# Two passes in one turn of the loop, with no barrier between them: counting semaphores, waits on the producers, and an order table over both passes

## The chip, the cores and the metric

The kernel runs on one core of one Trainium2 chip, in one launch. The metric is the device time in microseconds (us). The core's engines are named PE (TensorE, the matrix engine; its weight loads are PEld), DVE (VectorE), ACT (ScalarE), POOL (GpSimd) and SP (SyncE, which issues the DMAs here). Each engine runs its own stream of instructions in order and waits for the others by semaphores.

## The reference

The input is a batch of 32 independent samples of 256 tokens by 256 features, in float32. Each goes through two decoder layers, every sublayer behind a layer norm and added to the residual:

```
x = x + L0_attn (ln(x))                  # 16 heads of 16, low-rank k and v, rotary over heads   -> stream m
x = x + L0_xattn(ln(x), ctx, ctx)        # 16 heads of 64; softmax over the heads of a token     -> stream h
x = x + L0_ffn  (ln(x))                  # top half of the tokens by a router, FFN 1024, gate    -> stream h
x = x + L1_attn (ln(x))                  # 16 heads, keeps the top 25 of 256 scores of each row  -> stream t
x = x + L1_xattn(ln(x), ctx, ctx, lens)  # 16 heads of 16 over ctx, keys beyond lens masked      -> stream c
x = x + L1_ffn  (ln(x))                  # one product with a ternary weight                     -> stream c
```

## The kernel before, in words

All weights stay in SBUF. A sample (256 tokens by 256 features, two tiles of 128 tokens) passes through four **streams**, one per pass: m (attention of layer 0), h (cross attention over heads, router and FFN), t (the top-25 attention), c (masked cross attention, ternary FFN). A pass runs all four streams at once, each on another sample: m on i+3, h on i+2, t on i+1, c on i. With 32 samples there are 3 filling passes, 29 full ones in a loop of the hardware (`nc.Fori`, L1155), and 3 draining ones. The functions `tensor_h`, `vector_t`, `scalar_c`, `pool_m` and so on hold one engine's share of one stream, as Python generators with a `yield` at the points where another stream may come in. The function `woven` draws them together by a table of letters, `ORDER`, one string per engine: this table alone fixes the order of the instructions on each engine.

Within a pass the engines meet at named semaphores (`g["mla_x"]` is counted when stream m's residual is written, `spa_x` for stream t's, `md_x3` for stream h's, `lin_o` for stream c's). A pass ends with all engines at the end of an `nc.Block`, and a second block in which SP sets all the semaphores back to zero; a value waited for is the same in every pass. Streams hand samples on through buffers: m writes `xin`, which h reads next; h writes `xa`, which t reads next; t writes `x4`, which c reads next. Streams c and m share three PSUM banks (`bankM`) and the buffers of attention (`bufM`), so m follows c in a pass; h has `bankH`, t has `bankT`.

Lines used below: L299 transposes of a layer norm's output, L546 the projections of stream h (the first, `xwv`, from `ctxA`), L314 and L322 projections from and onto 256 features (`cwk`, `cwv` from `ctxB` are stream c's first, `swo` into `bankT` is stream t's last), L340 the scores, L350 their row maxima, L391/L394/L421 the transposed scores and values of streams m and c with the exponentials on ACT (L408), L883/L887 the 8-by-8 maxima and their removal (stream t's top 25), L863 the first DVE step of stream t after its layer norm, L529 the additions to the residual, L274/L278/L291 layer norm on DVE, L480 the reciprocals of a stream's attention sums, L1107 and L1145 the ends of the blocks.

## Time and profile before

| | us |
|---|---|
| median of 3 runs (6767.83, 6768.36, 6782.65) | 6768.36 |
| the profiled execution, its own time | 6756.82 |
| its span | 6755.0 |
| busy in that span: PE / DVE / ACT / POOL | 5896.7 / 4510.2 / 4012.6 / 1507.3 |
| mean granted clock of TensorE, as a share of 2.4 GHz | 0.899 |

Busy times overlap between engines. Busy PE is time in which a matmul was under way, whatever the clock; a matmul at the lower clock (1.2 GHz) counts longer. DMA hardly matters: 54.18 MB in the whole span, most at its start.

### The profile page before, as it was taken

To read this page: it belongs to the slowest core of one execution; us is meant where nothing else is said; L and a number is where in the kernel's file an instruction comes from. 1 tells how busy PE (TensorE), PEld (TensorE's weight loads), DVE (VectorE), ACT (ScalarE), POOL (GpSimd) and SP (SyncE) were. 2 spreads that over 40 slices of the span, in tenths; PEclk is the share of its full clock that TensorE was granted. 3 is DMA by queue.
4 is the path that set the end of the run, shared out by engine and by line. 5 is a ranking of instruction groups with operands and counts; after the bars stand their busy time and mean duration, and the time that the engine had idled before them with its cause. 6 is when DMAs were issued, how large, how long until landed. Compare 5 with 4: busy or idle time off the path is not lost. (4 is left out here: it accounts for less than half of the span.)

```text
span 6755.0 us, 109667 instructions
## 1 busy us (share of the span) xinstructions
PE 5896.7 (87%) x37509; PEld 3877.2 (57%) x37762; DVE 4510.2 (67%) x16186; ACT 4012.6 (59%) x9761; POOL 1507.3 (22%) x2564
## 2 busy tenths in 40 slices
PE   6888988988988988898888898888898898898876
PEld 3565565565565565565565565566556556556542
DVE  1366766666777666776676676666776666677653
ACT  2465666565666665666656566656566655566632
POOL 0122222222222222222222222222222222222211
PEclk7789989899999899999999899999998999999965
DMA  2000000000000000000000000000000000000000
GB/s 79 4 6 6 4 8 6 8 8 6 4 8 7 6 8 6 4 8 8 6 8 6 6 6 8 6 8 7 7 4 8 6 8 8 6 4 8 4 2 5
DMA packets 29456, 54.18 MB, mean 8 GB/s; under 512 B 8145, under 2 KB 9810, under 8 KB 27986
## 3 DMA queue, kind: packets, MB, share of 16 engines
q1 hardware_dynamic: 28770, 45.73, 2.1%
q8 instruction: 345, 5.65, 0.3%
q14 instruction: 341, 2.79, 0.1%
HBM read 37.33 MB, written 8.39 MB: 7 GB/s over the span
## 5 line engine op out<-in xcount | busy, mean ns | idle before, releaser
L914 POOL TENSOR_TENSOR t_pr<-t_pr,sc 128x512 f32<-128x512 f32 x512 | 649.6, 1269 | 1495.9 <-ACT t_pr L839 1495.9
L350 DVE TENSOR_REDUCE m_nm<-bankM 128x2 f32<-128x512 f32 x1024 | 657.0, 683 | 347.9 <-PE bankM L340 344.0
L887 DVE MATCH_REPLACE8 wk<-m,wk 128x256 f32<-128x256 f32 x2048 | 821.0, 408 | 0.0
L340 PE MATMUL bankM<-m_kT,m_q 32*128 32x256 f32 x4096 | 698.5, 466 | 75.4 <-DVE m_nm L350 74.3
L883 DVE MAX8 m<-wk 128x8 f32<-128x256 f32 x2048 | 759.2, 412 | 0.0
L651 ACT ACTIVATE xk_area<-bankH,xb 64x256 f32<-64x256 f32 x1024 | 480.7, 469 | 460.4 <-PE bankH L546 438.1
L394 PE MATMUL bankM<-m_q,m_kT 32*128 32x512 f32 x2048 | 627.9, 691 | 0.0
L883 DVE MAX8 m<-sc 128x8 f32<-128x256 f32 x1024 | 380.0, 412 | 327.5 <-ACT sc L830 290.1
L340 PEld LDWEIGHTS bankM<-m_kT,m_q 32*128 32x128 f32 x4096 | 411.3, 216 | 312.4 <-DVE m_nm L350 133.6
L845 ACT ACTIVATE t_pr<-t_pr,t_nm 128x256 f32<-128x256 f32 x1024 | 463.9, 504 | 182.5 <-POOL t_pr L914 180.5
L408 ACT ACTIVATE m_pT<-bankM,keymask 128x512 f32<-128x512 f32 x512 | 323.7, 683 | 247.4 <-PE bankM L394 247.4
L546 PE MATMUL bankH<-ctxA,xwv 128*128 128x256 f32 x1024 | 312.4, 467 | 166.2 <-issue 155.2
L445 ACT ACTIVATE t_pt<-bankT 128x512 f32<-128x512 f32 x512 | 307.5, 601 | 235.7 <-PE bankT L436 228.7
L391 PE MATMUL bankM<-m_m,sel_b 128*128 128x512 bf16 x865 | 301.2, 418 | 158.3 <-ACT m_pT L408 136.7
L436 PE MATMUL bankT<-ident,t_pr 128*128 128x128 f32 x2048 | 384.3, 318 | 55.4 <-ACT t_pr L845 54.3
L908 POOL TENSOR_SCALAR mx<-m 128x2 f32<-128x2 f32 x512 | 112.9, 221 | 1431.3 <-DVE wk L887 1421.1
L408 ACT ACTIVATE m_pT<-bankM 128x512 f32<-128x512 f32 x512 | 277.1, 593 | 235.3 <-PE bankM L394 235.3
L887 DVE MATCH_REPLACE8 wk<-m_last,wk 128x256 f32<-128x256 f32 x1024 | 410.5, 408 | 0.0
L887 DVE MATCH_REPLACE8 wk<-m,sc 128x256 f32<-128x256 f32 x1024 | 410.5, 408 | 0.0
L480 DVE RECIPROCAL m_rd<-bankM 128x16 f32<-128x16 f32 x128 | 23.6, 226 | 578.9 <-PE bankM L471 578.9
L436 PEld LDWEIGHTS bankT<-ident,t_pr 128*128 128x128 f32 x2048 | 262.7, 159 | 242.4 <-issue 142.2
L421 PE MATMUL bankM<-m_pT,m_va 128*32 128x256 f32 x4096 | 357.9, 423 | 42.6 <-ACT m_ot L428 41.2
(207 smaller groups left out, 12011.2 us busy)
## 6 DMA issues: line engine op xcount, KB each, us to landing
xin<-x_in SPq DMA_DIRECT2D x32, 256.0 KB, 2.6
ctxA<-ctx_in SPq DMA_DIRECT2D x32, 256.0 KB, 2.6
ctxB<-ctx_in SPq DMA_DIRECT2D x32, 256.0 KB, 3.5
out<-x SPq DMA_DIRECT2D x32, 256.0 KB, 2.0
w<-w_w SPq DMA_DIRECT2D x2, 1024.0 KB
xwq<-w_xwq SPq DMA_DIRECT2D x1, 1024.0 KB
xwk<-w_xwk SPq DMA_DIRECT2D x1, 1024.0 KB
xwv<-w_xwv SPq DMA_DIRECT2D x1, 1024.0 KB
```

What stands on the lines that cost most here:

```text
L340: last = nc.tensor.matmul(bank[x][:, j * S:(j + 1) * S], b["q2"][r:r + 32, e, j, t * P:(t + 1) * P], b["kT"][r:r + 32, e, :], start=not ma ...
L350: nc.vector.tensor_reduce(b["nm"][:, i % 2, 2 * (i // 2) + x, :], banks[u % 3][:].rearrange("p (j s) -> p j s", j=2), AX.X, ALU.max, negat ...
L394: nc.tensor.matmul(bank[x][:], b["kT"][r:r + 32, e, c * P:(c + 1) * P], b["q2"][r:r + 32, e].rearrange("p j s -> p (j s)"), start=False, s ...
L408: nc.scalar.activation(b["pT"][c][:, x, :], bank[x][:], ACT.Exp, bias=0.0 if bias is None else bias[:, c:c + 1]).then_inc(g[n + "_ex"], 1)
L421: last = nc.tensor.matmul(bank[r:r + 32, S * (m % 2):S * (m % 2 + 1)], b["va"][:, c, 4 * m + 2 * x + j, :], b["pT"][c][:, x, S * j:S * (j ...
L436: last = nc.tensor.transpose(bank[:, (2 * c + j) * P:(2 * c + j + 1) * P], b["pr"][:, u % 2, j, c * P:(c + 1) * P], w["ident"][:])
L546: last = nc.tensor.matmul(bankH[k % 2][:, hp * S:(hp + 1) * S], w[wt][:, d, c:c + P], src[:, d, :], start=(d == 0), stop=(d == ND - 1))
L651: nc.scalar.activation(dst[0:XD, :, 8 * h:8 * h + 8].rearrange("p (j a) u -> p j a u", a=2), bankH[k % 2][o * XD:(o + 1) * XD, hp * S:(hp ...
L845: nc.scalar.activation(b["pr"][:, u % 2, t, :], sp_[:, u % 2, t, :], ACT.Exp, bias=b["nm"][:, u, t:t + 1]).then_inc(g["spa_ex"], 1)
L883: link.inc(nc.vector.max(top, src[:, t, :]))
L887: m = nc.vector.match_replace(out=wk[:, k, t, :], in_to_replace=take, in_values=src[:, t, :], imm_value=-BIG)
L914: nc.gpsimd.tensor_tensor(sp_[:, u % 2], taken[:, u % 2], sc[:, u % 3], ALU.mult).then_inc(g["sp_mul"], 1)
```

## The change

The loop takes two passes per turn, 14 turns and one single pass after them in place of 29 turns. Between the two passes of a turn there is no block end, no clearing of semaphores and no branch. The semaphores count on through the turn: `at` adds to every value that is waited for the count of one pass (`COUNTS`) in the second lap, `past` makes an engine wait in the second lap for what the first must have finished before a buffer is written again. A generator is run twice in a row (`laps`), and the new `ORDER` covers both laps, so that one stream may be in its second lap while another is in its first. All single passes (the loop's rest, filling and draining) go by `ORDER_ONE`, a third table, also another order than before. The computing instructions are the same in kind and number.

```diff
@@ -56,20 +56,59 @@
+ORDER_ONE = {
+    "pe": runs("""
+        t h c m h2 c2 t h2 c t c t c t h c t h c h2 c h2 t c h3 t h t c t h c h t h c4 t c2 t c2 t h c2 h c t h c3 h c2 t h c t c t h c2 h t
...
+LAPS = 2
+COUNTS = dict(crs_ex=16, crs_k=1, crs_kT=1, crs_m3=1, crs_m3p=1, crs_nm=16, crs_on=2, crs_onT=1, crs_ont=1, crs_ot=2, crs_ott=1, crs_pv=8, crs_q=1,
...
+        lap = {"n": 0}
+        def name_of(s):
+            return next(n for n, x in g.items() if x is s)
+        def at(s, v):
+            return s, v + lap["n"] * COUNTS[name_of(s)]
+        def past(eng, *names):
+            for n in names:
+                if lap["n"]:
+                    eng.wait_ge(g[n], lap["n"] * COUNTS[n])
...
-            pool.wait_ge(g[f"ln{k}_stat"], 4)
+            pool.wait_ge(*at(g[f"ln{k}_stat"], 4))
...
+                if k == 0:
+                    past(pe, "md_x3", "ctxA_in")
...
+            past(dve, "mla_x", "md_x3")
...
+            past(dve, "md_x3", "spa_x")
...
-            pe.wait_ge(g["ctxB_in"], 16)
+            past(pe, "mla_x")
+            pe.wait_ge(*at(g["ctxB_in"], 16))
             project_T(bankM[0], w["cwk"], ctxB, g["crs_k"])
...
+            past(dve, "spa_x", "mla_x")
...
+        def laps(make, n):
+            for k in range(n):
+                it, more = make(), True
+                while more:
+                    lap["n"] = k
+                    more = next(it, END) is not END
+                    yield
         def woven(name, eng, streams):
-            for letter in ORDER[name]:
+            order = ORDER_ONE if lap["of"] == 1 else ORDER
+            for letter in order[name]:
                 if letter in streams:
                     next(streams[letter], END)
-        def one_pass(m=None, h=None, t=None, c=None, loaded=False):
+        def passes(n=1, m=None, h=None, t=None, c=None, loaded=False):
             there = {k: v is not None for k, v in (("m", m), ("h", h), ("t", t), ("c", c))}
             mode.update(there)
-            streams = lambda **all: {k: v for k, v in all.items() if there[k]}
+            lap["of"] = n
+            streams = lambda **all: {k: laps(v, n) for k, v in all.items() if there[k]}
             with nc.Block() as block:
                 @block.sync
                 def _(sp):
-                    if c is not None:
-                        sp.dma_start(ctxB[:], ctx_in[c]).then_inc(g["ctxB_in"], 16)
-                        sp.dma_start(lenb[:], lens_in[c]).then_inc(g["len_in"], 16)
-                    if m is not None:
-                        if h is not None:
-                            sp.wait_ge(g["hm_xb"], 1)
-                            sp.wait_ge(g["ln1_xn"], 2)
-                        if not loaded:
-                            sp.dma_start(xin[:], x_in[m]).then_inc(g["x_in"], 16)
-                        if h is not None:
-                            sp.wait_ge(g["hm_proj"], 12)
-                        sp.dma_start(ctxA[:], ctx_in[m]).then_inc(g["ctxA_in"], 16)
-                        sp.wait_ge(g["ctxA_in"], 16)
-                    if c is not None:
-                        sp.wait_ge(g["lin_o"], 1)
-                        sp.dma_start(out[c], x4[:]).then_inc(g["stored"], 16)
-                        sp.wait_ge(g["stored"], 16)
+                    for k in range(n):
+                        lap["n"] = k
+                        if c is not None:
+                            past(sp, "crs_k", "crs_v", "mask_row")
+                            sp.dma_start(ctxB[:], ctx_in[c + k]).then_inc(g["ctxB_in"], 16)
+                            sp.dma_start(lenb[:], lens_in[c + k]).then_inc(g["len_in"], 16)
+                        if m is not None:
+                            if h is not None:
+                                sp.wait_ge(*at(g["hm_xb"], 1))
+                                sp.wait_ge(*at(g["ln1_xn"], 2))
+                            if not loaded:
+                                sp.dma_start(xin[:], x_in[m + k]).then_inc(g["x_in"], 16)
+                            if h is not None:
+                                sp.wait_ge(*at(g["hm_proj"], 12))
+                            sp.dma_start(ctxA[:], ctx_in[m + k]).then_inc(g["ctxA_in"], 16)
+                            sp.wait_ge(*at(g["ctxA_in"], 16))
+                        if c is not None:
+                            sp.wait_ge(*at(g["lin_o"], 1))
+                            sp.dma_start(out[c + k], x4[:]).then_inc(g["stored"], 16)
+                            sp.wait_ge(*at(g["stored"], 16))
...
-                    woven("pe", pe, streams(t=tensor_t(pe), h=tensor_h(pe), c=tensor_c(pe), m=tensor_m(pe)))
+                    woven("pe", pe, streams(t=lambda: tensor_t(pe), h=lambda: tensor_h(pe), c=lambda: tensor_c(pe), m=lambda: tensor_m(pe)))
...
-        one_pass(m=0, loaded=True)
+        loops = (nb - 3) // LAPS
+        passes(m=0, loaded=True)
         setup_rest()
-        one_pass(m=1, h=0)
-        one_pass(m=2, h=1, t=0)
-        with nc.Fori(0, nb - 3) as i:
-            one_pass(m=i + 3, h=i + 2, t=i + 1, c=i)
-        one_pass(h=nb - 1, t=nb - 2, c=nb - 3)
-        one_pass(t=nb - 1, c=nb - 2)
-        one_pass(c=nb - 1)
+        passes(m=1, h=0)
+        passes(m=2, h=1, t=0)
+        with nc.Fori(0, loops * LAPS, LAPS) as i:
+            passes(LAPS, m=i + 3, h=i + 2, t=i + 1, c=i)
+        for i in range(loops * LAPS, nb - 3):
+            passes(m=i + 3, h=i + 2, t=i + 1, c=i)
+        passes(h=nb - 1, t=nb - 2, c=nb - 3)
+        passes(t=nb - 1, c=nb - 2)
+        passes(c=nb - 1)```

How the order moves, in three places. Names of lines have moved with the code: L299 is now L353, L314 L368, L322 L376, L340 L394, L350 L404, L394 L448, L391 L445, L421 L475, L436 L490, L456 L510, L471 L525, L493 L547, L546 L602, L529 L583, L863 L921, L883 L941, L887 L945, L1107 L1179.

PE, where a pass ends and the next begins; before, the loop's last and first rows (the loop comes back from L1155 to L1128):

```order
L493 MATMUL bankT<-ident,lnT_xn 128x128 x3
L322 MATMUL bankM<-wo,lnM_xT 128x256 [waits mla_onT]
L322 MATMUL bankM<-wo,lnM_xT 128x256 x3
L322 MATMUL bankT<-swo,lnT_xT 128x256 [waits spa_onT]
L322 MATMUL bankT<-swo,lnT_xT 128x256 x3
L1107 UNCONDITIONAL_BRANCH
```

```order
L1128 UNCONDITIONAL_BRANCH
L546 MATMUL bankH<-ctxA,xwv 128x256 x8
L314 MATMUL bankM<-ctxB,cwk 128x256 [waits ctxB_in]
L314 MATMUL bankM<-ctxB,cwk 128x256 x3
L322 MATMUL bankM<-cwv,ctxB 128x256 x4
L299 MATMUL bankT<-ident,lnT_xn 128x128 [waits ln3_xn]
```

The same place in the middle of a turn now:

```order
L376 MATMUL bankT<-swo,lnT_xT 128x256 [waits spa_onT]
L376 MATMUL bankT<-swo,lnT_xT 128x256 x3
L368 MATMUL bankM<-ctxB,cwk 128x256 [waits ctxB_in,mla_x]
L368 MATMUL bankM<-ctxB,cwk 128x256 x3
L376 MATMUL bankM<-cwv,ctxB 128x256 x4
L602 MATMUL bankH<-ctxA,xwv 128x256 [waits ctxA_in,md_x3]
L602 MATMUL bankH<-ctxA,xwv 128x256 x7
L353 MATMUL bankM<-ident,lnM_xn 128x128 [waits ln4_xn]
L353 MATMUL bankM<-ident,lnM_xn 128x128 x3
L353 MATMUL bankH<-ident,lnH_xn 128x128 [waits ln1_xn]
```

The branches and the barrier between `swo` and the next pass's projections are gone; the two projections are the same 16 matmul instructions, and stream c's layer norm is now transposed first.

DVE, from the layer norms at a pass's head to stream t's first maxima; before:

```order
L291 TENSOR_SCALAR lnM_xn<-x,lnM_mv,lnM_rs 128x256 [waits ln4_rstd]
L291 TENSOR_SCALAR lnM_xn<-x,lnM_mv,lnM_rs 128x256
L863 TENSOR_TENSOR t_va<-bankT,sbv 128x32x16 [waits spa_v]
L883 MAX m<-sc 128x8 [waits sp_sc]
L883 MAX m<-sc 128x8
```

Now, in a turn's second lap:

```order
L345 TENSOR_SCALAR lnT_xn<-xa,lnT_mv,lnT_rs 128x256 [waits ln3_rstd]
L345 TENSOR_SCALAR lnT_xn<-xa,lnT_mv,lnT_rs 128x256
L404 TENSOR_REDUCE m_nm<-bankM 128x2 [waits crs_s] x2
L921 TENSOR_TENSOR t_va<-bankT,sbv 128x32x16 [waits spa_v]
L404 TENSOR_REDUCE m_nm<-bankM 128x2 [waits crs_s] x2
L941 MAX m<-sc 128x8 [waits sp_sc]
L941 MAX m<-sc 128x8
```

Four of stream c's row maxima stand ahead of stream t's first step of top 25; before, none did.

PE, near the end of a pass, where streams m and t finish; before:

```order
L421 MATMUL bankM<-m_pT,m_va 32x256 [waits mla_ot,mla_ex]
L421 MATMUL bankM<-m_pT,m_va 32x256 x3
L391 MATMUL bankM<-m_m,sel_b 128x512 [waits mla_ex]
L391 MATMUL bankM<-m_m,sel_b 128x512
L394 MATMUL bankM<-m_q,m_kT 128x512 x2
L421 MATMUL bankM<-m_pT,m_va 32x256 [waits mla_ex]
L421 MATMUL bankM<-m_pT,m_va 32x256 x3
L391 MATMUL bankM<-m_m,sel_b 128x512 [waits mla_ex]
```

Now (first lap):

```order
L681 MATMUL bankH<-xv,w 128x128 [waits md_pickT]
L681 MATMUL bankH<-xv,w 128x128 x7
L475 MATMUL bankM<-m_pT,m_va 32x256 [waits mla_ot,mla_ex]
L475 MATMUL bankM<-m_pT,m_va 32x256 x3
L445 MATMUL bankM<-m_m,sel_b 128x512 [waits mla_ex]
L445 MATMUL bankM<-m_m,sel_b 128x512
L448 MATMUL bankM<-m_q,m_kT 128x512 x2
L687 MATMUL bankH<-w,xot 128x256 [waits md_hid] x4
L475 MATMUL bankM<-m_pT,m_va 32x256 [waits mla_ex]
L475 MATMUL bankM<-m_pT,m_va 32x256 x3
```

The FFN of stream h (L681 and L687, L625 and L631 before) has moved from the middle of the pass to its end, between stream m's last steps.

## Rows read from the trace of the kernel before

**Rows 1.** The page: busy time of the engines, and the maxima of streams c and m.

```profile
PE 5896.7 (87%) x37509; PEld 3877.2 (57%) x37762; DVE 4510.2 (67%) x16186; ACT 4012.6 (59%) x9761; POOL 1507.3 (22%) x2564
...
L350 DVE TENSOR_REDUCE m_nm<-bankM 128x2 f32<-128x512 f32 x1024 | 657.0, 683 | 347.9 <-PE bankM L340 344.0
```

**Rows 2.** Timeline of SP: a pass's first DMA (start us, us, engine line op, operands).

```profile
461.83 0.36 SPq L1111 DMA_DIRECT2D ctxB<-ctx_in  x1
...
1063.30 0.33 SPq L1111 DMA_DIRECT2D ctxB<-ctx_in  x1
...
1190.53 0.35 SPq L1125 DMA_DIRECT2D out<-x  x1
...
6087.58 0.33 SPq L1111 DMA_DIRECT2D ctxB<-ctx_in  x1
```

**Rows 3.** Timeline of PE where the loop comes back; idle before, and releaser, in brackets.

```profile
1059.29 1.89 PE L322 MATMUL bankT<-swo,lnT_xT 128*128 128x256 f32 x8
1066.48 5.95 PE L546 MATMUL bankH<-ctxA,xwv 128*128 128x256 f32 x16 [5.30 <-issue]
1072.27 1.89 PE L314 MATMUL bankM<-ctxB,cwk 128*128 128x256 f32 x8
1073.99 1.89 PE L322 MATMUL bankM<-cwv,ctxB 128*128 128x256 f32 x8
1075.72 0.60 PE L299 MATMUL bankT<-ident,lnT_xn 128*128 128x128 f32 x4
```

**Rows 4.** Timeline of DVE over the same stretch and on to stream t's first maxima.

```profile
1055.01 0.37 DVE L480 RECIPROCAL m_rd<-bankM 128x16 f32<-128x16 f32 x2 [14.92 <-PE bankM L471]
...
1059.49 0.69 DVE L529 TENSOR_TENSOR xin<-bankM,xin 128x512 f32<-128x512 f32 x1 [2.48 <-PE bankM L322]
1061.32 0.69 DVE L529 TENSOR_TENSOR x<-bankT,x3b 128x512 f32<-128x512 f32 x1 [1.13 <-PE bankT L322]
1066.50 0.75 DVE L274 BATCH_NORM_STATS2 lnT_st<-xa 128x6 f32<-128x256 f32 x2 [4.49 <-issue]
...
1074.15 0.74 DVE L291 TENSOR_SCALAR lnM_xn<-x,lnM_mv,lnM_rs 128x256 f32<-128x256 f32 x2 [0.46 <-POOL lnM_rs L286]
1085.43 0.69 DVE L863 TENSOR_TENSOR t_va<-bankT,sbv 128x512 f32<-128x512 f32 x1 [10.54 <-PE bankT L322]
1089.76 0.75 DVE L883 MAX8 m<-sc 128x8 f32<-128x256 f32 x2 [3.65 <-ACT sc L830]
```

**Rows 5.** Line L1155, the loop's branch on PE's queue (min/median/max ns).

```profile
L1155 PEldq COMPARE_BRANCH  x29: 79/3632/3980, 656.7 to 6285.7; - x29
```

**Rows 6.** Timeline of PE where the loop is first entered, by a barrier alone.

```profile
457.70 1.89 PE L322 MATMUL bankT<-swo,lnT_xT 128*128 128x256 f32 x8
...
461.37 3.69 PE L546 MATMUL bankH<-ctxA,xwv 128*128 128x256 f32 x16 [1.78 <-PEq L1145]
...
468.35 0.60 PE L299 MATMUL bankT<-ident,lnT_xn 128*128 128x128 f32 x4
```

**Rows 7.** Windows: us, then busy PE, PEld, DVE, ACT, POOL, then PEclk.

```profile
1170.00:1200.00 30.00, 26.04 (x192) 20.29 (x190) 25.96 (x97) 15.51 (x35) 10.65 (x20) 1.00 0.03 10
1200.00:1240.00 40.00, 37.52 (x228) 22.84 (x234) 33.68 (x120) 20.15 (x44) 6.93 (x14) 0.83 0.00 1
1240.00:1262.00 22.00, 16.41 (x122) 8.64 (x119) 3.39 (x10) 10.05 (x20) 1.97 (x4) 1.00 0.00 1
1337.00:1359.00 22.00, 21.78 (x88) 8.38 (x90) 13.25 (x56) 12.02 (x33) 3.98 (x7) 0.53 0.00 1
...
1261.50:1468.90 207.40, 185.83 (x1172) 121.53 (x1180) 140.48 (x505) 125.27 (x305) 47.20 (x80) 0.89 0.02 6
1063.30:1261.50 198.20, 176.99 (x1172) 117.34 (x1180) 140.56 (x505) 125.11 (x305) 47.08 (x80) 0.94 0.02 7
```

**Rows 8.** Timeline of PE near that pass's end: stream m's last steps.

```profile
1241.12 0.60 PE L391 MATMUL bankM<-m_m,sel_b 128*128 128x512 bf16 x2 [0.60 <-ACT m_pT L408]
...
1244.53 0.64 PE L421 MATMUL bankM<-m_pT,m_va 128*32 128x256 f32 x8 [1.16 <-ACT m_ot L428]
```

309 lines of the change are left out of this document (172 added, 137 removed).

## The prediction

> **What bounds the kernel now.** I read the page first: PE is busy 5896.7 us of the span, DVE 4510.2, the others less [rows 1], so the kernel runs at PE's pace, and what PE neither computes nor is fed is what a new order can win. Next SP's timeline, which marks where each pass begins: the first full pass starts at 461.83, the last at 6087.58, 28 turns in 5625.75 us, 200.9 us a turn [rows 2]. Then the windows over one turn of 198.2 us: PE is busy 176.99 us and stands idle 21.2 [rows 7]. The timeline of PE shows where the largest piece of that idle time is: where the loop comes back, the last product of stream t ends at 61.18 (1059.29 + 1.89), the next matmul starts at 66.48, 5.30 us idle with nothing the profile can name as releaser [rows 3]; DVE shows 4.49 us of the same [rows 4]. Two things lie in this gap. One is the barrier: where the loop is first entered, with the same blocks around but no branch back, PE idles only 1.78 us [rows 6]. The other is the branch: on PE's queue it takes 3632 ns in the median of 29, and 79 ns at least [rows 5]. 1.78 + 3.6 is 5.4, close to the 5.30.
>
> The Trainium skill (Runtime: NRT & Kernel Launch, section Instruction fetch mechanics) says that a taken branch to a target outside the fetched window makes the engine fetch that page before it goes on. The trace agrees: 3632 ns against 79.
>
> The gap also costs clock. The first 16 instructions after it take 5.95 us, while the next 8 take 1.89 at the full 2.4 GHz [rows 3]; at full speed the 16 would take 3.78, so 2.2 us more are lost. In all, from the end of `swo` to the first transpose of a layer norm the turn takes 1075.72 - 1061.18 = 14.5 us, in which PE does 3.78 + 1.89 + 1.89 = 7.6 us of work. At the entry without a branch the same stretch takes 468.35 - 459.59 = 8.8 us [rows 6].
>
> The rest of the turn's idle time, 21.2 - 5.3 = 15.9 us, is in small pieces of 0.3 to 1.4 us: 5.6 of it in the last 22 us of the pass and 4.0 in the 30 us from 1170 [rows 7]. Near the end PE waits for ACT between two exponentials, 0.60 and 1.16 us at a time [rows 8], and DVE waits 14.92 us before the sums of stream m are ready [rows 4]: streams m and t end there on their latencies, with little beside them.
>
> **The change part by part.** *The seam in the middle of a turn* (14 of them). The block ends, the clearing and the branch go. What is late next: the second pass's layer norms need stream t's result, which DVE ends at 1062.01 (1061.32 + 0.69) [rows 4], 0.8 us after PE. From the start of the layer norms to the end of stream c's normalised rows DVE takes 1074.15 + 0.74 - 1066.50 = 8.4 us [rows 4]. So the first transpose can start about 0.8 + 8.4 = 9.2 us after `swo`, while PE has the 7.6 us of projections to do, which need none of it. 14.5 - 9.2 = 5.3 us won per seam, with PE idle 1.6 us; if the norms were faster than before it would be 14.5 - 7.6 = 6.9 at most. The low end is that only the barrier goes, 1.8 us. I take 5.3, since its two terms are rows. 14 x 5.3 = 74 us. The clock's 2.2 us are in these 14.5 and are not counted again: an idle stretch of 1.6 us is no longer than those at 1241 to 1247, where the granted clock stayed at 1.00 [rows 7, 8].
>
> *Waits added by `past`.* PE's first projection waits for `mla_x`: DVE writes it at 1059.49 to 1060.18 [rows 4], while PE is in `swo` until 1061.18, so nothing. Behind it PE's whole queue stands; were it late, all of it would show. The `xwv` projection waits for `md_x3`, which the new order puts on DVE directly ahead of stream t's last addition; it is 3.8 us behind that point on PE, covered. DVE's first layer norm waits for `mla_x` and `md_x3`, both its own earlier work. SP's load of `ctxB` for the second lap waits for the store of the first: that store goes out at 1190.53, and the next pass needs the data at about 1072.27 + 198.2 = 1270.5 [rows 2, 3], some 80 us later. Cost of all four: 0; the worst I can bound is the 1.6 us of idle above, doubled. The end of each turn keeps barrier and branch: 14 gaps of 5.3 us stay, neither won nor lost.
>
> *The order inside a pass* (29 passes, two tables). The instructions are the same, so this term is how much of the 15.9 us of idle time per pass is filled, or added to. Two moves can be seen. Stream h's FFN goes from the middle to the end, between stream m's waits for ACT: of the 5.6 us idle there I take half, 2.8. Stream c's maxima go ahead of stream t's top 25: DVE waits 10.54 and 3.65 us at that place [rows 4], and four maxima of 683 ns [rows 1], 2.7 us, fit into it; this takes them out of the middle, where DVE is 87% busy (25.96 of 30 us) and PE idles 4.0 us [rows 7]. I take 1.2 of these. Together 4.0 us per pass. PE has the same projections ahead of stream t's first scores as before (the `xwv` pieces go back by as much as the scores of stream c come forward), so stream t's chain starts no later. Ends: above, all 15.9 us; below, a loss of 9.2 us, which is what a turn of 207.4 us costs over one of 198.2 with the same order [rows 7]. The value is nearer to the middle of these than to either, and rests on what I see covered. 29 x 4.0 = 116 us.
>
> *Filling and draining* (6 passes): with one to three streams there is little to interleave; 0.
>
> Sum against the profiled execution: 6756.8 - 74 - 116 = 6567 us. The median of the runs is 11.5 us above the profiled one's own time (6768.36 - 6756.82), so **6578 us**, 2.8% less.
>
> The body of the loop is twice as long now. I cost that at nothing: outside the branch PE's pieces of idle time have other engines as releasers [rows 8].
>
> The Trainium skill (TensorE: Matmul & The Clock Gate, section Part 1: The HAM clock gate) describes TensorE's clock as throttled by default and released by activity. The trace agrees at the gap. It does not by idleness alone explain the stretch from 1337 to 1359, where PE is busy 21.78 of 22 us and the clock is 0.53 [rows 7]. Under that rule the seams lose no clock, as in the sum.
>
> **The rivals.**
>
> A. *The order is worth nothing*, only the seams count: 6756.8 - 74 + 11.5 = 6694. For it: PE is already 89% busy in a turn (176.99 of 198.2) [rows 7] and the idle pieces are latencies between ACT and PE, which another order moves rather than removes. Against: the moved FFN is independent work, placed at exactly such waits.
>
> B. *The order packs much better*, 9 us per pass, more than half of the idle time, or some of it together with the low clock at 1200 to 1240 (0.83 [rows 7]): 6756.8 - 74 - 261 + 11.5 = 6433. For it: DVE has 14.92 idle at the end and 14.2 at the head to move work into. Against: streams m and t still end on the same chains.
>
> C. *The seam gives only the barrier's 1.8 us*, since the layer norms, the conversions on ACT and stream c's first scores are late one after another at the head, all moved forward in the order: 14 x 1.8 = 25, 6756.8 - 25 - 116 + 11.5 = 6627. Against: the entry without a branch reached the transpose after 8.8 us [rows 6].
>
> D. *Slower: the new order lowers the clock.* In the turn from 1261.5 PE ran at about half clock from 1337 to 1359, and the turn took 207.4 in place of 198.2 us [rows 7]; six of the 28 turns are of this length. The new order spreads stream h's small matmuls (64x128 and 128x128) and stream m's scores over a longer stretch without the dense projections. If every pass had such a stretch, 23 more would pay 9.2 us: 212 us, less the seams' 74, makes 6756.8 + 138 + 11.5 = 6906. It decides from a loss of 74 / 29 = 2.6 us per pass on. Against: the larger, weight-heavy products still come between, and 22 turns of 28 do without the long stretch.
>
> **How the numbers follow.** The forecast 0.41, A 0.19, B 0.18, C 0.07, D 0.11, and 0.04 that gains and losses cancel. 0.3%, 20 us, is about what a measurement of this kernel tells from no change. Faster: 0.41 + 0.19 + 0.18 + 0.07 = 0.85; same 0.04; slower 0.11. The likeliest case alone spans 2 us per pass with 4.3 per seam (6756.8 - 60 - 58 + 11.5 = 6650) to 7 us per pass with 6 (6756.8 - 84 - 203 + 11.5 = 6481). The range for 8 in 10 takes in A with some room, and B: 6430 to 6720; D lies outside.
>
> **What would show it.** In the changed profile: PE's idle time after stream t's `swo` product in the middle of a turn under 2 us and the next 16 projection instructions at 3.78 us; the branch on PE's queue 14 times at some 3.6 us; the distance of two such `swo` products, halved over a turn, near 200.9 - 4.0 - 2.7 = 194 us; PE's idle time in the last 22 us of a pass near 3 us. Wrong, if a turn of two passes takes over 402 us (the order loses), if the mean granted clock falls below 0.88 (D), or if PE idles more than 4 us at the seam, with DVE's layer norms as the releaser (C).

## The result, and the profile after

The changed kernel takes **6425.55 us** (median of 4 runs, 6419.66 to 6427.01), the kernel before 6775.5 beside it: 350 us less, a ratio of 0.9476, 95% interval 0.945 to 0.9502. The forecast was 6578, its range 6430 to 6720: the sign was right, the size was not, and the time lies just below the range.

The page of the changed kernel, its first and one later row (busy us and share of the span; then line, engine, operation, tiles, busy, mean ns | idle before). They answer to [rows 1]: PE is busy 164 us less, although it does the same work; the maxima cost what they did.

```profile
PE 5732.7 (89%) x37476; PEld 3762.5 (59%) x37762; DVE 4510.0 (70%) x16186; ACT 4001.4 (62%) x9761; POOL 1506.5 (23%) x2564
...
L404 DVE TENSOR_REDUCE m_nm<-bankM 128x2 f32<-128x512 f32 x1024 | 669.0, 682 | 454.9 <-PE bankM L394 454.6
```

SP's timeline, answering to [rows 2] (start, us, queue, line, operation, tiles): the first load of a turn, that of its second lap, the next turn's, and the single pass after the loop.

```profile
422.90 0.36 SPq L1186 DMA_DIRECT2D ctxB<-ctx_in  x1
...
532.17 0.34 SPq L1186 DMA_DIRECT2D ctxB<-ctx_in  x1
...
798.04 0.34 SPq L1186 DMA_DIRECT2D ctxB<-ctx_in  x1
...
5787.49 0.34 SPq L1186 DMA_DIRECT2D ctxB<-ctx_in  x1
...
5972.98 0.33 SPq L1186 DMA_DIRECT2D ctxB<-ctx_in  x1
```

14 turns take 5787.49 - 422.90 = 5364.6 us, 383.2 each, 191.6 a pass, in place of 200.9. So the span's 337.1 us (6755.0 - 6417.9) come from three places: the 29 full passes 5823.8 - 5550.1 = 273.8 (unrounded), the filling ahead of them 461.83 - 422.90 = 38.9, the draining behind them 24.4.

PE at the seam in the middle of a turn, answering to [rows 3] (start, busy, line, operation, tiles, count, idle before it and its releaser):

```profile
987.23 1.89 PE L376 MATMUL bankT<-swo,lnT_xT 128*128 128x256 f32 x8
988.96 1.89 PE L368 MATMUL bankM<-ctxB,cwk 128*128 128x256 f32 x8
990.68 1.89 PE L376 MATMUL bankM<-cwv,ctxB 128*128 128x256 f32 x8
992.41 3.62 PE L602 MATMUL bankH<-ctxA,xwv 128*128 128x256 f32 x16
996.59 0.66 PE L353 MATMUL bankM<-ident,lnM_xn 128*128 128x128 f32 x4 [0.56 <-DVE lnM_xn L345]
```

From the end of `swo` (989.12) to the first transpose it is 7.5 us, where it was 14.5; PE idles 0.56 us and both groups of 16 projections take 3.6 us: full clock.

The branch on PE's queue (duration min/median/max in ns), answering to [rows 5]:

```profile
L1232 PEldq COMPARE_BRANCH  x14: 79/3775/5147, 797.7 to 5787.5; - x14
```

The 79 ns are the last branch, which is not taken. So 28 branches were taken before and 13 are now: 15 are gone, one more than there are open seams, because the loop's last turn ends by a barrier alone.

The windows, answering to [rows 7] (stretch, length, busy us and instructions of PE, PEld, DVE, ACT, POOL; granted clock): the 28 passes of the loop, then the last 22 us of a turn.

```profile
422.90:5787.50 5364.60, 4930.08 (x32787) 3250.43 (x33038) 3931.23 (x14139) 3495.70 (x8540) 1317.70 (x2240) 0.93 0.02 7
1158.00:1180.00 22.00, 19.20 (x134) 12.54 (x133) 6.31 (x23) 11.22 (x25) 1.67 (x3) 1.00 0.01 1
```

PE idles 2.80 us in the last 22 us, where it idled 5.6 [rows 7]. Both windows reach past the end of `swo` (1177.8 now, 1259.4 before) into the gap at the turn's end, which holds 2.2 us of the 2.80 and 2.6 us of the 5.6. The 22 us up to the end of `swo`, before and now, have 3.41 and 0.60 us of idle time:

```profile
1237.40:1259.40 22.00, 18.59 (x151) 9.54 (x143) 3.63 (x14) 11.66 (x24) 2.90 (x4) 1.00 0.00 1
```

```profile
1155.80:1177.80 22.00, 21.40 (x154) 14.74 (x153) 7.79 (x31) 12.55 (x27) 2.81 (x4) 1.00 0.00 1
```

The same view of the kernel before over its first 28 turns:

```profile
461.80:6087.60 5625.80, 5030.26 (x32816) 3335.08 (x33038) 3934.32 (x14139) 3505.30 (x8540) 1319.05 (x2240) 0.93 0.02 7
```

Per pass PE idles (5364.60 - 4930.08) / 28 = 15.5 us, where it was (5625.80 - 5030.26) / 28 = 21.3. That is 5.8 us; the pass is 9.3 us shorter. For the rest I cut these 28 passes into slices of 10 us and summed length x (1 - granted clock) over them, which gives the time per pass that is lost if nothing but the clock counts. This **lost clock** is 14.7 us per pass before and 12.9 after. It also counts the low clock while PE stands idle, where it costs nothing; over PE's busy time alone it is 13.3 and 12.0.

The ends of the kernel, filling (from the load of `xin` at 125.5 and 124.7 on) and draining, before and now:

```profile
125.50:461.80 336.30, 276.33 (x1534) 192.90 (x1537) 151.30 (x536) 176.93 (x462) 55.16 (x88) 0.78 0.01 4
6285.70:6755.00 469.30, 346.84 (x1757) 201.86 (x1772) 258.08 (x948) 189.60 (x427) 81.81 (x143) 0.69 0.01 4
```

```profile
124.70:422.90 298.20, 248.98 (x1532) 177.03 (x1537) 152.75 (x536) 175.54 (x462) 55.43 (x88) 0.87 0.02 4
5973.00:6417.90 444.90, 320.07 (x1756) 192.39 (x1772) 259.19 (x948) 189.90 (x427) 81.82 (x143) 0.74 0.02 4
```

The two ends are 62.5 us shorter, and 54.1 us of that is PE's busy time for the same work at a higher clock (0.87 and 0.74, where it was 0.78 and 0.69). Idle time fell by 10.8 us in the filling and rose by 2.4 us in the draining.

The experiments are read by the same two numbers, idle time and lost clock:

| kernel (told below) | time, us | ratio to before | us per pass | PE idle | lost clock |
|---|---|---|---|---|---|
| before | 6756.8 (profiled) | 1 | 200.9 | 21.3 | 14.7 |
| **after** | 6425.6 | 0.9476 | 191.6 | 15.5 | 12.9 |
| one_lap | 6440.1 | 0.9520 | 192.1 | 19.8 | 9.7 |
| one_two_laps | 6404.7 | 0.9453 | 190.8 | 17.5 | 9.4 |
| pair_barrier | 6384.3 | 0.9426 | 190.1 | 17.8 | 8.0 |
| no_loop_barrier | 6347.4 | 0.9396 | 188.6 | 16.3 | 7.5 |
| old_two_laps | 6643.0 | 0.9818 | 196.4 | 17.6 | 12.3 |
| old_pair_barrier | 6678.7 | 0.9879 | 201.1 | 18.2 | 16.9 |
| old_ramp | 6492.8 | 0.9597 | 191.6 | 14.4 | 12.7 |
| x_c | 7688.5 | 1.131 | 232.5 | 40.5 | 32.0 |
| h_new_cm_old | 8383.2 | 1.232 | 256.3 | 53.6 | 51.1 |
| x_hc | 7745.2 | 1.126 | 236.9 | 42.7 | 39.9 |
| fill_before | 6711.2 | 0.9908 | 199.8 | 19.1 | 11.9 |
| fill_pair | 6338.5 | 0.9373 | 188.8 | 16.4 | 5.2 |
| fill_after | 6369.0 | 0.9378 | 189.6 | 12.6 | 9.7 |
| fill_no_loop | 6288.5 | 0.9284 | 186.7 | 14.9 | 3.6 |
| fill_laps28 | 6245.5 | 0.9222 | 185.8 | 10.1 | 7.8 |

Times are medians of 4 to 7 runs. The kernels ran in four groups, each beside runs of the kernel before: one_lap, one_two_laps, pair_barrier and old_two_laps beside 6775 us; no_loop_barrier, old_pair_barrier, old_ramp and fill_pair beside 6757; x_c, h_new_cm_old, x_hc and fill_after beside 6798; fill_before, fill_no_loop and fill_laps28 beside 6772. Across groups the ratios are to be compared. The last three columns are of the profiled execution, which in old_two_laps is 33 us below the median and in old_pair_barrier 75 us above it. Two of x_hc's four executions, the profiled one among them, ran slower at a lower granted clock, and its ratio is by the other two (7602.6 and 7700.5 us).

### The profile page after: what moved, and what is told of

Read it like the earlier page. It is cut to its first block and busy times, and to the rows that moved or that the text cites. A ratio compares the mean times of both kernels' runs of the same rounds, so it can differ in the third digit from the quotient of the medians.

```text
span 6417.9 us, 109223 instructions
## 1 busy us (share of the span) xinstructions
PE 5732.7 (89%) x37476; PEld 3762.5 (59%) x37762; DVE 4510.0 (70%) x16186; ACT 4001.4 (62%) x9761; POOL 1506.5 (23%) x2564
## 5 line engine op out<-in xcount | busy, mean ns | idle before, releaser
L404 DVE TENSOR_REDUCE m_nm<-bankM 128x2 f32<-128x512 f32 x1024 | 669.0, 682 | 454.9 <-PE bankM L394 454.6
L941 DVE MAX8 m<-wk 128x8 f32<-128x256 f32 x2048 | 756.3, 410 | 0.0
L448 PE MATMUL bankM<-m_q,m_kT 32*128 32x512 f32 x2048 | 685.6, 750 | 0.0
L394 PE MATMUL bankM<-m_kT,m_q 32*128 32x256 f32 x4096 | 613.7, 419 | 35.5 <-DVE m_nm L404 28.2
L462 ACT ACTIVATE m_pT<-bankM,keymask 128x512 f32<-128x512 f32 x512 | 323.7, 683 | 314.6 <-PE bankM L448 313.9
L394 PEld LDWEIGHTS bankM<-m_kT,m_q 32*128 32x128 f32 x4096 | 369.4, 193 | 230.1 <-issue 145.7
L941 DVE MAX8 m<-sc 128x8 f32<-128x256 f32 x1024 | 380.7, 413 | 105.4 <-ACT sc L887 76.3
L772 DVE TENSOR_REDUCE xnm<-bankH 128x4 f32<-128x512 f32 x256 | 175.6, 686 | 386.7 <-PE bankH L636 386.4
L445 PE MATMUL bankM<-m_m,sel_b 128*128 128x512 bf16 x835 | 307.7, 435 | 153.7 <-ACT m_pT L462 81.2
L490 PE MATMUL bankT<-ident,t_pr 128*128 128x128 f32 x2048 | 358.8, 302 | 57.6 <-ACT t_pr L902 57.1
L462 ACT ACTIVATE m_pT<-bankM 128x512 f32<-128x512 f32 x512 | 282.4, 592 | 201.1 <-PE bankM L448 201.1
L636 PE MATMUL bankH<-xk_area,xq_area 72*128 72x128 f32 x2048 | 342.3, 320 | 49.1 <-ACT xk_area L707 48.5
L475 PE MATMUL bankM<-m_pT,m_va 128*32 128x256 f32 x4096 | 361.9, 434 | 24.1 <-ACT m_ot L482 18.0
L636 PEld LDWEIGHTS bankH<-xk_area,xq_area 72*128 72x128 f32 x2048 | 303.0, 227 | 134.9 <-issue 68.5
L941 DVE MAX8 m_last<-wk 128x8 f32<-128x256 f32 x1024 | 379.3, 412 | 0.0
```

Source lines behind the costliest of these rows:

```text
L394: last = nc.tensor.matmul(bank[x][:, j * S:(j + 1) * S], b["q2"][r:r + 32, e, j, t * P:(t + 1) * P], b["kT"][r:r + 32, e, :], start=not ma ...
L404: nc.vector.tensor_reduce(b["nm"][:, i % 2, 2 * (i // 2) + x, :], banks[u % 3][:].rearrange("p (j s) -> p j s", j=2), AX.X, ALU.max, negat ...
L448: nc.tensor.matmul(bank[x][:], b["kT"][r:r + 32, e, c * P:(c + 1) * P], b["q2"][r:r + 32, e].rearrange("p j s -> p (j s)"), start=False, s ...
L462: nc.scalar.activation(b["pT"][c][:, x, :], bank[x][:], ACT.Exp, bias=0.0 if bias is None else bias[:, c:c + 1]).then_inc(g[n + "_ex"], 1)
L475: last = nc.tensor.matmul(bank[r:r + 32, S * (m % 2):S * (m % 2 + 1)], b["va"][:, c, 4 * m + 2 * x + j, :], b["pT"][c][:, x, S * j:S * (j ...
L490: last = nc.tensor.transpose(bank[:, (2 * c + j) * P:(2 * c + j + 1) * P], b["pr"][:, u % 2, j, c * P:(c + 1) * P], w["ident"][:])
```

## Experiments on the order and the seam

Four kernels separate the table for one pass from the crossing of passes. **one_lap** is the changed kernel with one pass per turn:

```diff
-LAPS = 2
+LAPS = 1
```

> One pass per turn again (29 turns, barrier and branch after each), every pass by ORDER_ONE, so only the order tables differ from the kernel before. Theory (order): the changed profile splits the 337 us into 63 in filling and draining, about 14 x 7.1 = 99 at the seams, and the rest, some 185 us or 6.4 us per pass, in the order inside a pass. Then this kernel takes about 6775 - 63 - 185 = 6527 us (6505 to 6550), a turn of the loop about 194.5 us in place of 200.9. Rival (crossing): the gain inside the loop comes from streams crossing the seam, and the order in a closed pass is worth at most 1 us: 6775 - 63 - 29 = 6683 or more, a turn near 200 us.

6440.07 us (6436.12 to 6474.41), ratio 0.952 [0.9488, 0.9553]: 335 of the 350 us without a single open seam. Both theories had it too slow; the order had been taken far too small.

**old_two_laps** has the table of before, twice over, with the seam in the middle open:

```diff
-ORDER_ONE = {...}
+ORDER_ONE = that of before, each engine
-ORDER = { "pe": runs("""h m t c h2 ...   # two laps, crossing
+ORDER = { "pe": runs("""t h c m h2 ...""") * 2   # that of before, each engine
```

> The order table of the kernel before, written twice as the table of a turn of two passes, counting semaphores and no barrier in the middle; single passes by the old table. Only the seam differs from the kernel before. Theory (order): a seam is worth what it saves in PE's way from the last product of stream t to the first transpose, about 6 to 7 us, whatever the table: 6775 - 14 x 6.5 = 6684 us (6670 to 6700). Rival (crossing): with the old table the engines still stand at the seam for each other's tails, and only the barrier's 1.8 us go: 6775 - 25 = 6750.

6643.03 us (6609.58 to 6666.18), 0.9818 [0.9795, 0.9842]. In the old order 14 open seams, with the fifteenth branch that goes as well, are worth 132 us, 9.5 per seam: more than the 5.3 of the forecast. At the seam itself PE reaches the first transpose 6.7 us after `swo` without any idle time.

**one_two_laps** has `ORDER_ONE` twice over as the two-lap table:

```diff
-ORDER = { "pe": runs("""h m t c h2 ...
+ORDER = ORDER_ONE of each engine, twice
```

> The changed kernel, but with ORDER_ONE written twice as the table of a turn, so that no stream crosses the seam. Theory (order): the same as the changed kernel within 0.5%, 6425 us (6400 to 6460), since the table of two laps is worth no more than the one-lap table twice. Rival (crossing): slower by 2 us or more per pass, 6483 or more.

6404.67 us (6393.9 to 6413.58), 0.9453 [0.9434, 0.9473]. The planned two-lap table is no better than the one-pass table repeated (0.9476); the intervals overlap. It buys 2.0 us of idle time per pass and pays 3.5 us of lost clock.

**pair_barrier** keeps the barrier and the clearing in the middle, only the branch goes:

```diff
-            passes(LAPS, m=i + 3, h=i + 2, t=i + 1, c=i)
+            for j in range(LAPS):
+                passes(m=i + j + 3, h=i + j + 2, t=i + j + 1, c=i + j)
```

> Two passes per turn, but each its own block with barrier and clearing of semaphores between them, by ORDER_ONE; against one_lap only 14 of 29 branches are gone (the body is twice as long). Theory (branch): the branch is most of the gap; a boundary without it took 8.8 us from the last product to the first transpose in place of 14.5: 14 x 5.7 = 80 us less than one_lap, within 25 us of one_two_laps. Rival (barrier): the barrier and the clearing hold half of it or more, so only 14 x 3 = 42 us less than one_lap.

6384.31 us (6383.52 to 6387.71), 0.9426 [0.9411, 0.9442], the best so far and faster than the changed kernel. Against one_lap 15 taken branches are gone (28 to 13; the expectation counts 14) and 56 us with them, 3.7 each. Against one_two_laps the barrier is back, and the kernel is 20 us *faster*: with `ORDER_ONE` an open seam is worth nothing beyond its branch. The open seam itself is shorter, 8.5 us from `swo` to the transpose against 9.3 to 9.5 with the barrier; but one_two_laps loses 1.4 us more clock per pass.

The barrier without the branch, on PE, in this kernel (PEq is PE's sequencer):

```profile
987.63 1.99 PE L376 MATMUL bankT<-swo,lnT_xT 128*128 128x256 f32 x8 [0.69 <-ACT lnT_xT L553]
991.31 3.04 PE L602 MATMUL bankH<-ctxA,xwv 128*128 128x256 f32 x13 [1.69 <-PEq L1221]
```

1.69 us, as at the loop's entry [rows 6], against 5.30 with the branch.

**old_pair_barrier** asks the same in the old order (the table of before and the edit above).

> Every pass (filling and draining too) by the order table of the kernel before, every pass closed by its barrier and clearing as before, but two passes written out per turn of the loop: only 14 of 29 branches go (15 remain with the single pass's absence, 14 turns). Theory 'branch': in the order of before a seam without barrier and branch was worth 132 us in all (6775 to 6643); if that is the branch (its 3.6 us and the half-clock stretch that follows the gap, 2.2 us), this kernel has most of it: 14 x 5.8 = 81 us, about 6694. Rival 'barrier': what counts is that the second pass starts while the first ends; then this one gains only what the branch gave under the new order, 4.0 us each, 56 us: about 6719 or later. Rival 'nothing': branch time was hidden, 6775.

6678.71 us (6671.09 to 6753.9), 0.9879 [0.9841, 0.9916]: 78 us for 15 branches, 5.2 each, near what 'branch' said. The other 54 us of old_two_laps' 132 are then its 14 barriers, 3.9 each. By the ratios it is 2.9 each, and the two intervals touch, so this part is less certain. Its profiled execution is its longest run, 6753.9: idle time fell to 18.2 us per pass there and lost clock rose to 16.9, which took the gain back. That run's mean granted clock was 0.891, that of the four others (6671 to 6688 us) 0.901 to 0.904: one kernel's runs can differ by 80 us together with their clock.

**no_loop_barrier** writes out 28 closed passes (`LAPS = 28` with the loop of pair_barrier).

> The new table for a closed pass (ORDER_ONE) in all 29 full passes, each with its barrier and clearing, 28 of them written out in one turn of the loop: no branch between passes. With one branch per pass 6440, with one per two passes 6384. Theory 'branch costs 4.0 us each': 6440 - 28 x 4.0 = 6328. Rival 'long code': instructions that run only once must be brought in as they are reached, which costs as much as the branches or more: 6384 or above.

6347.42 us (6343.29 to 6376.73), 0.9396 [0.9352, 0.9439]. Between the two: the last 13 taken branches gave 0.3% over pair_barrier (20 us by the ratios, 37 by the times, so 1.6 to 2.8 each), less than the first 15, and within the overlap of the intervals. Straight code costs nothing that shows.

**old_ramp** gives the filling and draining passes back their old table:

```diff
-            order = ORDER_ONE if lap["of"] == 1 else ORDER
+            order = (ORDER_ONE if len(streams) == 4 else ORDER_OLD) if lap["of"] == 1 else ORDER
```

> The changed kernel, but the filling and draining passes (one to three streams) by the order table of the kernel before; the loop and its single rest pass unchanged. In the profiles the two ends of the kernel were 38.9 and 24.4 us shorter after the change. Theory 'order': that is the new table, so this kernel takes 6426 + 63 = 6489. Rival: it is the semaphores or the code around, 6426; or the table acts on the filling alone, 6426 + 39 = 6465.

6492.84 us (6480.21 to 6501.13), 0.9597 [0.9559, 0.9636]: 67 us more than the changed kernel by the times, 82 by the ratios. The gain at the ends of the kernel is the new table's, as 'order' said. Its first full pass starts at 467.2, that of the changed kernel at 422.9, and its draining takes 470.2 us in place of 444.9.

Three kernels tried to split the one-pass table: streams named new stand where `ORDER_ONE` has them, counted in stream t's steps, the others where the table of before has them.

```diff
-LAPS = 2
+LAPS = 1
-ORDER_ONE = {...}
+ORDER_ONE = the table of before, with the letters c (x_c), h (h_new_cm_old) or h and c (x_hc) moved
```

> One pass per turn with barrier and branch, as in the kernel before, all passes by one table: streams t, h and m at the places of the table before, stream c's steps at the places (counted in stream t's steps) that ORDER_ONE gives them. Table before, all streams: 6757 to 6775 (turn 200.9 us); ORDER_ONE, all streams: 6440 (turn 191.2). If moving c (its maxima ahead of stream t's top 25) carries half of what the prediction took for the order: 1.2 of 4.0 us per pass, about 6720. If it is what keeps the clock up (the second low stretch, 140 to 160 us into the pass, gone): the turn near 195, 6600. If it collides with the rest, later than 6760.

> The same with only stream h's steps moved to the places of ORDER_ONE (its FFN at the end of the pass), c and m where the table before has them. The prediction gave this move 2.8 us per pass: about 6675. Theory 'clock': the low stretch 140 to 160 us into each pass of the table before (about 7 us of full clock lost per pass) goes when the FFN stands beside stream m: turn near 194 us, 6560. Rival: h and c only fit together, here 6760 or later.

> The same with streams h and c both at the places of ORDER_ONE and m where it was before. If the moves of h and c add up to the whole, this is ORDER_ONE's 6440. If stream m's places carry the rest, it lies between 6440 and the better of the two kernels that move one stream. Rival: 6600 or later, m's move being what makes room.

7688.46, 8383.19 and 7745.2 us; ratios 1.1311 [1.1269, 1.1353], 1.2315 [1.2251, 1.2378], 1.126 [1.1161, 1.1359]. The collision that two of the expectations allowed for came, far larger than any number in them. Idle time rises to 1.9 to 2.5 times that of before, lost clock to 2.2 to 3.5 times (the profiled execution of x_hc, 7815.8 us, is its longest). Which move inside the table brings the gain stays open; these edits could not tell.

## Experiments on the clock

What the closed pass gained is mostly clock: from before to one_lap the lost clock falls by 5.0 us per pass (by 6.1 over PE's busy time alone) and idle time by 1.5, of 8.8. Where the clock falls in one_lap can be read in PE's timeline (a pass that starts at 1007.2) and in its windows:

```profile
1064.99 0.39 PE L427 MATMUL bankM<-ident_b,m_sp 128*24 128x128 bf16 x4
1067.04 0.60 PE L445 MATMUL bankM<-m_m,sel_b 128*128 128x512 bf16 x2 [1.66 <-ACT m_m L434]
1067.57 1.13 PE L448 MATMUL bankM<-m_q,m_kT 32*128 32x512 f32 x4
1070.05 1.03 PE L445 MATMUL bankM<-m_m,sel_b 128*128 128x512 bf16 x2 [1.35 <-ACT m_pT L462]
1071.01 2.08 PE L448 MATMUL bankM<-m_q,m_kT 32*128 32x512 f32 x4
1073.02 1.08 PE L475 MATMUL bankM<-m_pT,m_va 128*32 128x256 f32 x8
```

```profile
1063.00:1066.00 3.00, 2.38 (x16) 1.71 (x13) 3.00 (x14) 2.93 (x7) 1.81 (x7) 1.00 0.00 0
1066.00:1069.00 3.00, 1.66 (x6) 0.41 (x6) 3.00 (x13) 1.23 (x3) 0.87 (x1) 0.94 0.32 93
1069.00:1071.00 2.00, 0.95 (x2) 0.13 (x2) 2.00 (x10) 2.00 (x5) 0.40 (x2) 0.50 0.00 0
...
1073.00:1076.00 3.00, 3.00 (x18) 1.46 (x18) 3.00 (x13) 1.86 (x3) 0.00 (x0) 0.58 0.00 0
1076.00:1079.00 3.00, 2.65 (x32) 1.03 (x32) 0.00 (x0) 1.44 (x3) 0.00 (x0) 1.00 0.00 0
```

PE waits 1.66 us for `m_m` and 1.35 us for the first exponentials; the clock is at 1.2 GHz from about 1068.6 to 1075.5, in which four L448 take 2.08 us in place of 1.13. The second fall, about 103 us into the pass, stands behind a wait of 2.63 us for `t_pr`. The third is the loop-back. This is the pattern of 24 of the 28 passes; in two others (from 611.2 and 2154.2) the first fall lasts 37.5 us, and the pass takes 204 in place of 191 us.

If the clock costs time by itself, work put into such a wait must make the kernel *faster*. **fill_pair** is pair_barrier with 11 products per pass whose results are overwritten:

```diff
@@ at_scores_T
             yield
+            if n == "crs" and i < 2:
+                for _ in range(6 - i):
+                    nc.tensor.matmul(bank[2 * i][:], ident_b[:], sel_b[:, 0:4, :].rearrange("p k c -> p (k c)"), start=True, stop=True,
+                                     skip_group_check=True)
             if i == 0:
                 pe.wait_ge(*at(g[n + "_m3"], 1))
```

> The closed pass by ORDER_ONE, two passes written out per turn with a barrier between (6384 without the additions), with 11 extra 128x512 bf16 matmuls per pass whose results are overwritten: 6 ahead of stream c's first transposed scores (PE is idle 1.66 us there), 5 ahead of its second (1.35 us idle). Nothing else is changed. Theory 'clock': the pass loses time because the granted clock falls to half for some 6.7 us after those two waits (about 60 us into each pass); with PE busy there it does not fall, and 2 to 4 us of each of 29 passes come back: 6268 to 6326. Rival 'latency': the time of the pass is set by waits, the clock is a by-product: 6384, or up to 11 x 0.2 us x 29 = 64 us later where the additions delay PE: 6384 to 6448.

6338.53 us (6335.65 to 6345.23), 0.9373 [0.9338, 0.9409]: 46 us less by the times, 36 by the ratios, with 352 matmuls *more*. PE's timeline there shows five of them in place of the wait, and L452 (the old L448) at 1.13 us:

```profile
1420.16 1.25 PE L442 MATMUL bankM<-sel_b,ident_b 128*128 128x512 bf16 x5
1421.57 0.60 PE L449 MATMUL bankM<-m_m,sel_b 128*128 128x512 bf16 x2 [0.16 <-ACT m_pT L466]
1422.11 1.13 PE L452 MATMUL bankM<-m_q,m_kT 32*128 32x512 f32 x4
1423.17 0.64 PE L479 MATMUL bankM<-m_pT,m_va 128*32 128x256 f32 x8
```

Two like passes, of pair_barrier and of fill_pair: clock 0.97 and 0.99, 187.4 and 185.3 us.

```profile
1370.80:1558.20 187.40, 170.36 (x1180) 113.16 (x1180) 140.88 (x505) 124.51 (x305) 47.38 (x80) 0.97 0.02 7
```

```profile
1363.30:1548.60 185.30, 169.94 (x1191) 113.09 (x1191) 140.65 (x505) 124.45 (x305) 47.27 (x80) 0.99 0.02 7
```

Lost clock went from 8.0 to 5.2 us per pass, the pass from 190.1 to 188.8: about half of what the clock gives back reaches the end, and the time is 12 us past the late end of what 'clock' had forecast. No kernel has the same products at a place that no fall follows, so that it is the place that counts is not shown.

**fill_after** and **fill_before** put the same edit into the changed kernel and into the kernel before. The slices of 10 us that the expectations name give the granted clock from the start of a pass on.

> The changed kernel with 11 extra 128x512 bf16 matmuls per pass in two waits of stream c (6 before its first transposed scores, 5 before its second), their results overwritten. In the closed passes this took the low stretch 60 us into the pass away and 46 us off the time. The changed kernel has that stretch in each first lap (80, 50, 66 in three slices of 10 us) and one of 73, 50, 75 in each second lap, there behind a wait of 2.14 us for ACT's xk_area, to which nothing is added. Theory 'clock': the first-lap stretch goes, some 9 us at half clock, 3 to 4 us per turn, perhaps part of the second: 6426 - 14 x 3.5 = 6377 or less. Rival 'latency' : 6426 to 6490.

> The kernel before, unchanged but for 11 extra 128x512 bf16 matmuls per pass in two waits of stream c (6 before its first transposed scores, 5 before its second), their results overwritten. Before: a low stretch begins behind these waits some 75 us into each pass, short in 22 turns (slices of 10 us at 0.83 or 0.87) and 20 us long in the others (0.79, 0.50, 0.69). Theory 'clock': it goes, the turns of 207 us become 198, and 1.7 us come back in the rest: 6 x 9 + 23 x 1.7 = 93 us, 6775 - 93 = 6682; the stretch 140 to 160 us into the pass stays. Rival 'latency': 6775 to 6775 + 29 x 2.3 = 6840, since the first of the two waits is shorter here (0.16 us) and the additions delay PE.

fill_after: 6368.95 us (6355.29 to 6381.96), 0.9378 [0.9338, 0.9418], 57 us less by the times, 66 by the ratios. fill_before: 6711.23 us (6698.45 to 6722.84), 0.9908 [0.9882, 0.9935], 61 us less than the runs beside it. 'Clock' holds in both orders. In fill_before the stretch behind these waits is gone from every pass, and the longest pass takes 201.5 us in place of 207.4; two thirds of the expected 93 us came back. In fill_after another stretch, 27 us long, begins some 120 us into the turn in 10 of 14 turns, while PE is still in the first lap (slices of 0.51, 0.50, 0.63 from 1283); in the changed kernel only 4 turns have it. What is saved at one fall is in part lost at another. In the ten us ahead of that stretch (it begins at 1283.2) PE waits 0.42 us at most:

```profile
1280.01 1.13 PE L394 MATMUL bankM<-m_kT,m_q 32*128 32x256 f32 x8 [0.18 <-DVE m_nm L404]
1281.07 1.16 PE L640 MATMUL bankH<-xk_area,xq_area 72*128 72x128 f32 x8
1282.65 1.60 PE L394 MATMUL bankM<-m_kT,m_q 32*128 32x256 f32 x8 [0.42 <-DVE m_nm L404]
```

**fill_no_loop** and **fill_laps28** look for the best kernel: both write out 28 passes and have the 11 products, the first closed by barriers in `ORDER_ONE`, the second without any seam, in the changed kernel's two-lap table 14 times over.

```diff
-LAPS = 2
+LAPS = 28
-ORDER = {...}
+ORDER = the two-lap table of each engine, 14 times   # fill_laps28 alone
```

> All 28 passes written out, by ORDER_ONE, each with its barrier and without a branch, with the same 11 extra matmuls. Without them 6347 (beside 6757 for the kernel before), with them and 14 branches 6339. If both gains add up: 6347 - 29 x 1.6 = 6300, passes of 185.5 us throughout, as those that no branch precedes with the additions. Rival: now and then a pass falls into the long stretch (a pass of 192.7 us was seen): 6330.

> The changed kernel's two-lap table fourteen times over in one stretch of 28 passes without barrier, clearing or branch between any of them, with the same 11 extra matmuls. With the extra matmuls, a turn of two passes with its loop-back takes 365 to 389 us (mean 379); without any loop-back 14 x (11 to 15) us should go: 6369 - 14 x 12 = 6200 if the crossing of passes is worth anything by itself. Rival: the table crosses the seams well only where it was planned to (the middle of a turn), the low stretches 20 us long stay: 6300 or above, no better than closed passes without branches.

6288.49 us (6282.37 to 6289.72), 0.9284 [0.9242, 0.9326], and **6245.53 us** (6237.01 to 6267.34), 0.9222 [0.9174, 0.927]: the fastest, 180 us below the changed kernel. The first is near the 6300 forecast; against no_loop_barrier its products are worth 59 us by the times and 76 by the ratios, with 3.6 us of lost clock per pass in place of 7.5. The second lies between its two theories: with no loop-back left the crossing table is at last worth more than closed passes, and PE idles only 10.1 us per pass; but it loses 7.8 us per pass of clock against 3.6. Two passes of one pair of fill_laps28:

```profile
1272.50:1479.20 206.70, 196.79 (x1222) 127.31 (x1222) 145.40 (x528) 128.92 (x314) 48.24 (x81) 0.88 0.02 6
1479.20:1655.20 176.00, 166.14 (x1163) 110.39 (x1164) 135.58 (x485) 121.10 (x297) 45.92 (x79) 0.98 0.02 7
```

The second does nearly the same work in 176.0 us at 0.98; the first, at 0.88, holds two stretches at half clock. This pair takes 382.7 us, 19.8 of it idle. Another two passes with the same instructions ran at 1.00:

```profile
2590.60:2948.80 358.20, 337.65 (x2383) 223.43 (x2383) 280.47 (x1013) 249.83 (x611) 94.18 (x160) 1.00 0.02 7
```

They take 358.2 us, 20.6 of it idle. All of the 24.5 us between them is PE's busy time, and the two differ in nothing but the clock that the views show.

## Why the prediction missed

*What bounds the kernel.* Right: PE. The kernel was won by idle time and clock of PE, no other engine's work changed. Of the span's 337 us, 173 are PE's idle time, 100 the low clock while PE is busy, and 64 PE's busy time at equal clock.

*The seam* (14 x 5.3 = 74 us). The mechanism held in each of its parts: 7.5 us from `swo` to the transpose (9.2 forecast), PE idle 0.56 us (under 2), 16 projections at full clock, branch 14 times. DVE took 6.7 us (989.87 to 996.53) from its first layer norm to the end of stream c's rows, less than the 8.4 taken from the old order. One of its reasons was misread: the waits at 1241 to 1247 are 0.60 and 1.16 us, so 1.6 us is longer than they are. The clock did stay at 1.00, behind 0.56 us here and behind 1.69 us in pair_barrier. What did not hold is that the seam is worth the same in any order: 9.5 us per seam with the old table (5.2 for a branch, some 3 to 4 for a barrier), 3.7 less 1.5 with `ORDER_ONE`, and 1.0 in the changed kernel against one_lap (14.5 us over 14, a fifteenth branch among them). The terms were added as if independent; alone the new order gives 335 us and the open seam 132, a sum of 467, and together they give 350. The 1.8 us that rival C allowed the seam are nearer to what it was worth behind the new order, but not for C's reason: the layer norms were not late, PE waited 0.56 us for them.

*Waits added by `past`*: nothing, as said. SP's second-lap load goes out at 915.79, PE needs it at 988.96.

*The end of a turn*: neither won nor lost at 13 of the 14, as said, with a branch of 3775 ns in the median. The fourteenth has no taken branch, and PE's gap there is 2.1 us.

*The order inside a pass* (29 x 4.0 = 116 us). **This is the step that failed.** By the runs it is 335 - 67 = 268 us, 9.2 per pass. The term counted idle time alone and was bounded by the 15.9 us of it; only rival B named the low clock. The 14.7 us per pass that the granted clock cost were to be read in the page of before and in the windows (the stretch at 0.53 [rows 7]), but stood in no term. In the closed pass of one_lap the clock gives 6.1 of the 8.8 us (over PE's busy time), idle time at most 1.5 where 4.0 were forecast, and 1.2 are left. ("At most", because some 8 of 1180 PE records per pass are missing in the trace of before and none in that of one_lap, and a missing record can count as idle time.) In the changed kernel it is 1.3, 5.8 and 2.2 of 9.3: its fuller order fills more and, with its own falls, keeps less of the clock. So for the order by itself the clock is what was missing; in the changed kernel's loop, order and seam together, idle time and clock gave the 7 us per pass that the forecast had for both (4.0 + 2.7), and the excess is the 2.2 us of PE's busy time at equal clock, whose cause stays open.

The number of the first move came out by luck. PE's idle time in the last 22 us went from 5.6 to 2.8, by the 2.8 that were taken, but 2.6 of the 5.6 were the gap at the turn's end, which the sum had counted already as part of its 5.3. Up to the end of `swo` there were 3.41 us, and 2.8 of them were filled: nearly all, not half. What stream c's move was worth is not shown.

*Filling and draining* (0). **This term failed too**: it was put at nothing because there is little to interleave, and it is 63 us in the traces, 67 to 82 in old_ramp. Again it is the clock: 54 of the 62.5 us are PE's busy time for the same work at a higher clock, and in the draining passes idle time did not fall. The filling also moves earlier: in its second pass the load of `xin` for the third (it waits for stream h's layer norm) went out at 285.49 before and at 254.82 after.

*The rivals.* B's sum, 6433, is close, and its mechanism (9 us per pass, idle time and low clock together) is what the order did; the seams' 74 us in it are too much and the ends' 63 are missing, which cancel by luck. A is refuted by one_lap. D is refuted as a sum (the clock rose from 0.899 to 0.914), yet its mechanism is real in the two-lap table: 12.9 us of lost clock per pass against 9.4 with `ORDER_ONE` twice. The range ended 4 us too high because it gave B no room below.

## What to carry to other kernels

Before forecasting an order, sum (1 - granted clock) over slices of the kernel before: here it came to two thirds of PE's idle time per pass, and at the kernel's ends it was the larger of the two (221 us of lost clock, 182 idle). Don't add the gain of an open seam to that of a better order without a run that has one of them alone: here 132 and 335 us gave 350. Write a pair of passes out first and see what the branch alone gives. Where PE has to wait in the middle of its work and the clock falls behind that wait, a few products into a bank that is overwritten anyway can be worth more than they cost.
